# Moving the bounds of the expert lists behind the last output, and the low part ahead of the counts

## The reference

```python
x = X
x = x + 0.5 * ffn(layernorm(x))       # stage "1" of the kernel
x = x + attention(layernorm(x))       # stage "at"
x = x + 0.5 * ffn(layernorm(x))       # stage "2"

def ffn(inp):                                        # inp: [4096, 256]
    x = w_norm * inp * rsqrt(mean(inp**2) + 1e-6)
    probs = softmax(x @ w_router)                    # 32 experts
    w, sel = top_k(probs, 4)                         # each token goes to 4 experts
    # every expert takes at most 128 of its tokens, in order of the token's number
    for e in range(32):
        rows = first_128(tokens with e in sel)
        out[rows] += probs[rows, e] * ((silu(x[rows] @ w_gate[e]) * (x[rows] @ w_up[e])) @ w_down[e])
    shared = silu(x @ sw_gate) * (x @ sw_up) @ sw_down   # 704 wide, for all tokens
    return inp + out + sigmoid(x @ w_shared_gate) * shared
```

## Time and profile before

| what | us |
|---|---|
| three runs | 983.84, 981.41, 984.94 |
| median | 983.84 |
| the profiled execution, its own time | 983.84 |
| span of its instructions | 982.1 |
| TensorE matmul busy in the span | 918.9 (94%) |
| VectorE busy | 689.8 (70%) |
| ScalarE busy | 534.5 (54%) |
| GpSimd busy | 501.7 (51%) |

### The profile page before, as it was taken

How to read it: one execution, slowest core, us unless ns; L and a number is a source line. 1 busy time by engine, 2 the same in 40 slices (tenths; PEclk the granted TensorE clock), 3 DMA queues, 4 the chain that set the end, 5 groups by cost and what they waited for, 6 DMA issues and landing times.

```text
span 982.1 us, 18325 instructions
## 1 busy us (share of the span) xinstructions
PE 918.9 (94%) x6274; PEld 686.1 (70%) x6274; DVE 689.8 (70%) x1702; ACT 534.5 (54%) x798; POOL 501.7 (51%) x534
## 2 busy tenths in 40 slices
PE   1999999999999999999999999878999999999997
PEld 1778886777778765666666666436888867777786
DVE  4988777644444768998998999757887786444435
ACT  3667652233233477888888887665676522332322
POOL 5342112565553376887887887634421125565530
PEclk9999999999999999999999999889999999999999
DMA  6433316677774510001001001004323166777835
GB/s 195 123 95 99 102 47 183 168 181 181 173 185 84 177 66 22 23 30 34 22 22 43 21 11 65 12 11 131 108 90 94 61 186 167 179 183 179 187 42 170
DMA packets 95433, 101.91 MB, mean 104 GB/s; under 512 B 18688, under 2 KB 86656, under 8 KB 95360
## 3 DMA queue, kind: packets, MB, share of 16 engines
q1 hardware_dynamic: 83072, 83.17, 27.7%
q0 software_dynamic: 12288, 17.83, 10.8%
HBM read 65.44 MB, written 35.54 MB: 103 GB/s over the span
## 4 chain that ended last, share of the span: by engine, by line
PE 44%; DVE 13%; issue 4%; POOL 2%; ACT 2%; DMA 0%; DVEq 0%; POOLq 0%; ACTq 0%; SPq 0%
PE gu L86 4%; PE zT L966 4%; PE gu L87 3%; PE gu L88 3%; PE pj_at L86 3%; PE pv_at L1617 3%; PE gu L986 3%; PE pj_at L87 3%; PE pj_at L88 3%; PE scores_at L1601 2%; PE down L86 2%; PE down L88 2%; PE down L87 2%; PE den_at L1633 2%; DVE both_at L1842 2%
## 5 line engine op out<-in xcount | busy, mean ns | idle before, releaser
L86 PE MATMUL gu<-x_hi,gu_hi 128*128 128x512 f32 x264 | 121.7, 461 | 3.3 <-DVE act_gu L1236 3.3
L1708 ACT ACTIVATE capped_at<-scores_at 128x2048 f32<-128x2048 f32 x64 | 93.3, 1458 | 32.1 <-PE scores_at L1601 31.9
L758 POOL DMA_INDIRECT rows<-z_rows,slots x64 | 68.7, 1073 | 72.7 <-DVE slots L1227 53.7
L88 PE MATMUL gu<-x_lo,gu_hi 128*128 128x512 f32 x264 | 104.6, 396 | 0.0
L87 PE MATMUL gu<-x_hi,gu_lo 128*128 128x512 f32 x264 | 104.5, 396 | 0.0
L1044 ACT CAST a_hi<-act_gu 128x512 fp32r<-128x512 f32 x96 | 59.2, 616 | 82.7 <-DVE act_gu L1236 70.2
L1716 ACT ACTIVATE probs_at<-capped_at 128x2048 f32<-128x2048 f32 x64 | 95.2, 1487 | 2.5
L1784 POOL TENSOR_SCALAR_AFFINE_SELECT probs_at<-probs_at 128x1024 f32<-128x1024 f32 x64 | 85.8, 1345 | 17.8 <-ACT probs_at L1716 17.1
L86 PE MATMUL down<-down_hi,a_hi 128*128 128x256 f32 x300 | 93.8, 313 | 0.2 <-DVE a_lo L1246 0.2
L1119 ACT ACTIVATE y<-gu,rows 128x256 f32<-128x256 f32 x64 | 30.4, 474 | 110.3 <-PE gu L986 106.9
L966 PE MATMUL zT<-w_gu,xT 128*128 128x352 f32 x256 | 87.1, 463 | 0.0
(11 more groups left out here) (245 smaller groups left out, 2596.1 us busy)
## 6 DMA issues: line engine op xcount, KB each, us to landing
w_gu<-in_w_gate SPq DMA_DIRECT2D x64, 176.0 KB, 2.6
w_gu<-in_w_up SPq DMA_DIRECT2D x64, 176.0 KB, 3.2
w_down<-in_w_down SPq DMA_DIRECT2D x64, 176.0 KB
z_rows<-z SPq DMA_DIRECT2D x16, 512.0 KB, 3.1
acc<-base SPq DMA_DIRECT2D x10, 512.0 KB, 3.5
out<-base SPq DMA_DIRECT2D x10, 512.0 KB, 3.4
x_f<-in_X SPq DMA_DIRECT2D x8, 512.0 KB, 4.6
xn_at<-acc SPq DMA_DIRECT2D x16, 256.0 KB, 2.7
```

The costliest lines, as they stand in the source:

```text
L86: nc.tensor.matmul(out, w_hi, x_hi, start=first, stop=False)
L88: return nc.tensor.matmul(out, w_hi, x_lo, start=False, stop=last)
L1708: nc.scalar.activation(capped[:, u % 2, :, 0:n], scores[:, :, 0:n], ACT.Tanh, scale=QK_SCALE / SOFTCAP).then_inc(capped_ready, 1)
```

## The change

It reorders, in both FFN stages, instructions on TensorE and VectorE. No instruction is added or taken away.

1. In each of the slots 0 to 3 `take_counts(r)` goes from ahead of the last low part (`a_lo_part(b, 5)`) to behind it.
2. `tile_starts` goes from ahead of the last tile of slot 3's down projection to behind it, at the head of the lead.
3. `list_bounds` goes from ahead of slot 3's last output (`outputs(3, 1)`) to behind it, and `list_tiles` behind the product of followup 4.
4. In the lead, find(0) and find(1) stand behind 7 pieces (before: 6), find(2) behind 11 (10), find(3) behind 13 (14). On VectorE the lists 0 and 1 stand together behind followup 6, ahead of the product of followup 8; list 2 ahead of followup 11, list 3 ahead of followup 13.

```diff
@@ slot, TensorE
                 for j in range(TJ):
-                    if s is None and j == TJ - 1:
-                        tile_starts()
                     down_proj(b, j, range(MT))
@@ lead, TensorE
             def lead():
-                for p in range(0, 6):
+                tile_starts()
+                for p in range(0, 7):
                     piece(p)
                 find(0)
                 find(1)
-                for p in range(6, 10):
+                for p in range(7, 11):
                     piece(p)
                 find(2)
-                for p in range(10, 14):
+                for p in range(11, 13):
                     piece(p)
                 find(3)
-                for p in range(14, LEAD):
+                for p in range(13, LEAD):
                     piece(p)
@@ slot, VectorE (the same swap in slot_behind)
                 product(b, 5)
+                a_lo_part(b, 5)
                 take_counts(r)
-                a_lo_part(b, 5)
...
                 weigh(r)
                 if s is not None:
                     statistics(s + 2)
-                else:
-                    list_bounds()
                 outputs(b, 1)
-                if s is None:
-                    list_tiles()
@@ lead, VectorE
             def lead():
+                list_bounds()
                 for p in range(0, 5):
                     followup(p)
+                list_tiles()
+                for p in range(5, 7):
+                    followup(p)
                 list_experts(0)
-                for p in range(5, 9):
-                    followup(p)
                 list_experts(1)
-                for p in range(9, 13):
+                for p in range(7, 11):
                     followup(p)
                 list_experts(2)
-                for p in range(13, 17):
+                for p in range(11, 13):
                     followup(p)
                 list_experts(3)
-                followup(17)
+                for p in range(13, LEAD):
+                    followup(p)
```

More of the change, by code:

```diff
@@ L1335, in slot_behind @@
                 product(0, 5)
+                a_lo_part(0, 5)
                 take_counts(r)
-                a_lo_part(0, 5)
                 statistics(s + 1)
```

## The result

The changed kernel took 991.01 us in the median of five runs (989.30 to 991.21), the kernel before 983.07 in five runs beside it (981.41 to 984.94): a ratio of 1.007 with a 95% interval of 1.0056 to 1.0085, slower. Its profiled execution took 988.74 us with a mean granted clock of 0.987; the one of before took 983.84 at 0.989.

What follows compares the result with a forecast made beforehand. TensorE was taken to set the pace, with VectorE's queue setting the lead's end; 2.8 us lost in each of two stages, 5.6 in all, on 983.84 gave 989.4 us, range 986.0 to 992.5.

Steps and rivals of the forecast that it cites:

- Swap: Slots 0 to 3, counts behind the low part: 0 us, at most 1.8; late tile_starts hides later rank loads.
- VectorE's idling: Ahead of slot 3's second output half, VectorE idles from 145.42 to 147.54 for the down projection: 2.1 us lost.
- First wait: In the lead, TensorE waits 1.1 us ahead of find(0), until 153.6, for the later in_tile_ready.
- Second wait: In the lead, TensorE waits 2.0 us ahead of piece 10, until 158.4, for followup 8's product behind lists 0 and 1.
- The end of the lead: Copy of expert 0's rows at 166.4, 2.75 us later; turn_rows(1) at 167.2, before 164.41.
- The two ScalarE waits: In the lead, VectorE's low part waits for ScalarE's high part, 0.8 us after followup 11's product and at the last pair.
- Stage 2: Stage 2's turn_rows(1) comes near 809.8, that is 804.21 + 5.6.
- The clock: Four lead waits where two were; about one half-speed drop, already in the time: nothing added, 1.3 down and 2.6 up in range.
- The room: Rival: TensorE's 2.08 us idling at turn_rows(1) absorbs the loss if the copy comes by 163.7; 983.8 to 982; chance 0.06.
- Idling alone: Rival: only VectorE's idling counts, ScalarE's high parts being covered; 2.4 us in all, 986.2; chance 0.10.
- More half speed: Rival: two or more of the four lead waits drop the clock beyond today's one; 992.0; chance 0.12.
- The rows landed in time: Rival denied: late gathers, landing 3 us over 7.6, make turn_rows(1) 1.9 us later per stage; 993.2; chance 0.04.

Runs made afterwards that it cites:

- no swap: The changed kernel with take_counts again ahead of the last low part in all slots: 990.68 us against 986.18, ratio 1.0062.
- the swap alone: The kernel before with only take_counts moved behind the last low part: 989.45 us against 982.48; again in 12 runs, 987.46 against 984.49.
- the repeat: The changed kernel, unaltered, run once more against the kernel before: 990.62 us against 984.49, ratio 1.0074.
- the full version: Kernel before with two more gate/up pieces in the lead, copy_rows(0) ahead of list 3, weight loads from expert 2 on held back: 977.49 us, again 979.15.
- bounds late: Kernel before with only tile_starts and list_bounds at the head of the lead and list_tiles behind followup 4: 991.82 us against 982.48.
- putting the bounds back: Changed kernel with tile_starts, list_bounds and list_tiles back in slot 3, leaving the swap and regrouped finds and lists: 990.94 us against 982.48.

## Why the prediction was right, point by point

The forecast was 989.4; the changed kernel took 991.01 in the median beside the kernel before, and 990.17 in the mean of all 28 executions, 5.5 us above before where 5.6 had been worked out (the two medians taken beside each other are 7.9 apart). That the sum agrees to 0.1 us is in part luck, as the last points below show. To compare times within the traces I take off 0.14 us, the shift of the mark.

- **Swap.** Nothing was forecast; with tile_starts late it costs nothing (no swap: 27.26, with it: 27.28 in the same clock). Right, and for the reason given: the swap alone showed the one us per us of a lost cover, 0.76 and 0.86 us of TensorE's wait. From the mark tile_starts stands at 6.35 in the changed kernel, and the rank loads released it at 5.26 in the swap alone: 1.1 us to spare, 0.8 forecast. The 1.8 us allowed for the slots don't show: the mark is 0.14 later. What failed was my later expectation for the swap alone, which took the whole edit as free and left this cover out.
- **VectorE's idling.** 2.1 us until 147.54 forecast; 2.16 us and 147.58 measured.
- **First wait.** 1.1 us, find(0) at 153.6; measured 0.99 and 153.61.
- **Second wait.** 2.0 us, 158.4; measured 1.90 and 158.42, released by the product. Right.
- **The end of the lead.** The copy at 166.4 and turn_rows(1) at 167.2 were forecast; the profiled execution has 167.50 and 168.26. This is the step that was off, by 1.1 us. The two ScalarE waits are there, with 0.69 us each of idling. What the working hadn't got are VectorE's waits of 0.52 and 0.33 for find(2) and find(3), which come late because TensorE runs at half speed from 158 to 163. In the execution without it neither of these two waits appears, turn_rows(1) is 26.34 us behind the mark, and the forecast was 167.2 - 140.98 = 26.2. So the queue was worked out to 0.1 us, and the clock was missing from it.
- **Stage 2.** 809.8 forecast, 809.17 measured. Nearly right by terms that cancel: 0.94 too little in each lead for the clock, 1.3 given back behind turn_rows(1) of stage 1, and 1.5 between there and the mark of stage 2.
- **No room behind the lead.** "Nothing behind it has room to give it back" was wrong for stage 1: 0.72 us of the delay is taken up in the wait at the stage's end. It is not steady, as this wait is 1.89 in the repeat. From mark to mark the changed kernel is 1.01 and 1.95 us longer than before, from the mark of stage 2 to the end of the span 3.75 and 2.87. In stage 2 the premise holds.
- **Expert rows.** VectorE's copy, and no gather, releases turn_rows(1) in each stage. Right.
- **The clock.** "Two in seven of four is about one", hence nothing added. The profiled execution had two drops in the leads, both behind the second wait and none at turn_rows(1), and one less in attention: a sum near nothing, by other terms than mine, and so by luck. Over all executions the changed kernel's mean clock is 0.9869 and that of before 0.9872. So adding nothing was right to within 0.3 us (0.0003 by the slope).
- **The rivals.** The room did not swallow it: the copy came 3.8 us later and not by 163.7. Idling alone would be a lead of 24.6, and 26.34 was measured. More half speed (992.0) was part of the profiled execution's leads, but was offset elsewhere. The rows landed in time:

GpSimd's gather of expert 1 in the changed kernel, and the landing of the two gathers issued from 158 to 159.6 (the number behind the count is us):

```profile
158.60 1.01 POOL L758 DMA_INDIRECT rows<-z_rows,slots  x1 [0.30 <-issue]
```
```profile
rows<-z_rows,slots POOLq DMA_INDIRECT x2, 5.0
```

The issue takes 1.01 us as before, with 0.30 ahead of it, and landing is sooner than the 7.6 us of before. The blocking that the Trainium skill describes (SBUF — State Buffer, SBUF: two separate sides) doesn't show here beside a VectorE that was busy for 12.6 of 14.4 us. But the VectorE row beside this gather is a low part, and no run varied which form stands there, so the rule itself isn't tested.

What stays open: why one and the same wait is followed by half speed in one execution and not in another, what makes the load at the end of stage 1 come later in some executions, and whether the 0.9 us that the full version gains beyond its 3.6 is more than the error of the times.

## What to carry to other kernels

On an engine that others wait for, put work that needs nothing new into the gap ahead of an instruction that must wait; moving it behind that instruction costs the whole gap, and each group of work put together then shows as a wait of whoever needs the item behind it. An edit that is free in one order can be on the path in another, so name its cover and look whether the cover is part of the same change. Where the clock varies, compare kernels by a distance within the trace and by many executions brought to equal clock, and distrust an interval from four runs.

## What the runs showed of the hardware

- Waits of 1.8 to 2.2 us were followed by half speed in some executions of a program and by full clock in others: 27.28 against 26.34 us for the same lead, and 26.83 against 25.28 in the two stages of one trace.
- Behind turn_rows(1), half speed stood in 7 of 8 leads with a wait of 1.90 to 2.19 us there and in none of 12 with 1.19 to 1.67; each such stretch made the next step 6.1 us long in place of 4.8.
- The mean granted clock of an execution varied from 0.983 to 0.992 in the kernel before, and the time by 9 us with it, about -0.77 us for +0.001.
- TensorE, busy for 94% of the span, was not the bound everywhere: at the end of stage 1 it waited 0.98 us (before) and up to 4.15 us (the full version again) behind a load that VectorE needed.
- Taking parts of a change out one by one misled where another part was their cover: bounds late cost 1.84 us a stage, yet putting the bounds back left the lead at 27.35, since it laid bare the 0.9 us of the swap.
